# First attention of a four-layer block: the product of cosines and sines with the exponentials, on GpSimd or on VectorE

## What is computed

```python
p_w = exp(clip(score_scale * s_raw, -20, 20) + log_tw)     # per batch, position, channel
phi = k_val[..., None] * theta                             # 8 angles (M) per channel
re_k, im_k = cos(phi), sin(phi)
den    = cumsum(p_w, axis=1)                               # along the positions
num_re = cumsum(p_w[..., None] * re_k, axis=1)
num_im = cumsum(p_w[..., None] * im_k, axis=1)
...
out = sum over M of (num_re * A + num_im * B) / den        # A, B: from the queries
y   = silu(out * ...) @ W_out
```

## Time and profile before

| | |
|---|---|
| median of 3 runs | 1704.63 us (1704.37 to 1704.65) |
| the profiled execution, its own time | 1704.6 us |
| its span (first to last instruction) | 1702.8 us |
| VectorE busy over the span | 1182.2 us (69%) |
| TensorE busy, matmuls | 1216.5 us (71%) |
| ScalarE busy | 771.0 us (45%) |
| GpSimd busy | 417.0 us (24%) |

### The profile page before, as it was taken

How to read it: one execution, slowest core, us unless ns; L and a number is a source line. 1 busy time by engine, 2 the same in 40 slices (tenths; PEclk the granted TensorE clock), 3 DMA queues, 4 the chain that set the end, 5 groups by cost and what they waited for, 6 DMA issues and landing times. The chain is left out here.

```text
span 1702.8 us, 27530 instructions
## 1 busy us (share of the span) xinstructions
PE 1216.5 (71%) x8838; PEld 870.2 (51%) x8838; DVE 1182.2 (69%) x3159; ACT 771.0 (45%) x1217; POOL 417.0 (24%) x627
## 2 busy tenths in 40 slices
PE   2666566899986777755676774776665999967776
PEld 1555444788873333355343442665554344446665
DVE  4998899666666777544777675767874566647776
ACT  3334533233333766654466662433332466633333
POOL 3433443100003333011354431112220222100000
PEclk9888878899995999978789886878887799979998
DMA  7000000000000000000000000000000000000000
GB/s 279 1 0 0 0 0 0 1 0 0 0 0 1 2 0 1 2 0 0 1 1 0 1 1 0 1 0 0 1 0 1 1 2 0 2 1 0 0 0 25
DMA packets 5674, 13.83 MB, mean 8 GB/s; under 512 B 224, under 2 KB 4448, under 8 KB 5088
## 3 DMA queue, kind: packets, MB, share of 16 engines
q1 hardware_dynamic: 5600, 12.92, 2.0%
HBM read 11.88 MB, written 1.05 MB: 8 GB/s over the span
## 5 line engine op out<-in xcount | busy, mean ns | idle before, releaser
L1694 DVE TENSOR_REDUCE mx<-PS 128x2 f32<-128x512 f32 (+1 forms) x256 | 155.1, 620 | 82.7 <-PE PS L944 73.2
L359 POOL TENSOR_TENSOR tve<-tmv,eps 128x2 f32<-128x2 f32 x64 | 16.2, 253 | 720.3 <-DVE tmv L1480 719.1
L616 ACT ACTIVATE w_l0f<-PS 128x512 f32<-128x512 f32 (+1 forms) x256 | 137.3, 543 | 102.7 <-PE PS L951 100.4
L775 ACT ACTIVATE sg<-PS 128x512 f32<-128x512 f32 (+1 forms) x104 | 60.3, 580 | 201.0 <-PE PS L1391 200.7
L1391 PE MATMUL PS<-hT,w_l0f 128*128 128x256 f32 x512 | 121.4, 383 | 0.0
L870 PE MATMUL PS<-cb,w_const 128*128 128x256 f32 x128 | 44.6, 481 | 98.4 <-DVE sbuf L1620 98.3
L2101 DVE TENSOR_TENSOR y<-sg,PS 128x512 f32<-128x512 f32 (+1 forms) x104 | 69.2, 666 | 55.4 <-ACT sg L775 43.1
L815 PE MATMUL PS<-w_const,h 128*128 128x128 f32 x128 | 31.3, 331 | 98.2 <-DVE h L1471 88.6
L1391 PEld LDWEIGHTS PS<-hT,w_l0f 128*128 128x128 f32 x512 | 94.2, 193 | 10.8
L1320 PE MATMUL PS<-w_l2f,y 128*128 128x128 f32 x512 | 77.3, 300 | 10.3 <-ACT y L733 6.9
L1320 PEld LDWEIGHTS PS<-w_l2f,y 128*128 128x128 f32 x512 | 75.1, 216 | 17.9 <-ACT y L733 9.8
(11 more groups left out here) (369 smaller groups left out, 3348.1 us busy)
## 6 DMA issues: line engine op xcount, KB each, us to landing
w_l0f<-in_l0f SPq DMA_DIRECT2D x1, 3076.0 KB, 13.8
w_l2f<-in_l2f SPq DMA_DIRECT2D x1, 2214.0 KB, 19.8
w_l3f<-in_l3f SPq DMA_DIRECT2D x1, 1736.0 KB, 23.5
w_l0a<-in_l0a SPq DMA_DIRECT2D x1, 1093.0 KB, 7.9
result<-X SPq DMA_DIRECT2D x1, 896.0 KB, 4.6
X<-in_x SPq DMA_DIRECT2D x1, 768.0 KB, 10.2
w_l1f<-in_l1f SPq DMA_DIRECT2D x1, 582.0 KB, 15.5
PT<-in_cbf SPq DMA_DIRECT2D x1, 576.0 KB, 11.1
```

What stands on the lines that cost most here:

```text
L616: act.activation(P8[:, hh % 8, 0:width], PS[:, hh % 2, 0:width], ACT.Exp, scale=SM_SCALE).then_inc(a["pt"], 1)
L775: act.activation(sg[:, c % 2, 0:cols], gate, func).then_inc(f["sg"], 1)
L1694: dve.tensor_reduce(mx[:, hh, 0:nm], PS[:, 2 + hh % 2, 0:nm * keys].rearrange("p (t k) -> p t k", t=nm), AX.X, ALU.max).then_inc(a["mx"], 1)
```

## The change

GpSimd's loop for the first attention keeps only the two deviations. The two products of a chunk go to the head of VectorE's `cumulate`, which now waits for `a_trig` (and, for chunk 0, for `a_p`) instead of `a_pp`, issues the two products, raises `a_pp` itself (ScalarE still waits for it before it overwrites `pw`), and drains before the scans.

```diff
                 with pool.Fori(0, NB) as i:
                     if l == L0_ATTN:
-                        for c in range(CHUNKS):
-                            pool.wait_ge(a_trig, i * CHUNKS + (c + 1))
-                            if c == 0:
-                                pool.wait_ge(a_p, i + 1)
-                            for b in (cb, sbuf):
-                                ins = pool.tensor_tensor(b[:, c], b[:, c],
-                                                         pw[:].unsqueeze(1).to_broadcast([P, CHUNK_M, L]), ALU.mult)
-                            ins.then_inc(a_pp, 1)
-                            if c == 1:
-                                head_rstd(i + (head0[l] + 2))
+                        head_rstd(i + (head0[l] + 2))
                     tail_rstd(i + (tail0[l] + 1))
...
                     def cumulate(u, c):
-                        dve.wait_ge(a_pp, u * CHUNKS + (c + 1))
+                        dve.wait_ge(a_trig, u * CHUNKS + (c + 1))
+                        if c == 0:
+                            dve.wait_ge(a_p, u + 1)
+                        for b in (cb, sbuf):
+                            ins = dve.tensor_tensor(b[:, c], b[:, c],
+                                                    pw[:].unsqueeze(1).to_broadcast([P, CHUNK_M, L]), ALU.mult)
+                        ins.then_inc(a_pp, 1)
+                        dve.drain()
                         cf = carry[:].rearrange("p m t -> p (m t)")
```

## The result

| | before | after |
|---|---|---|
| median | 1704.68 us (15 runs, 1703.97 to 1709.90) | 1709.69 us (15 runs, 1702.92 to 1715.27) |
| ratio to before, 95% interval | | 1.0024 [1.0013, 1.0035] |
| profiled execution, its own time | 1704.6 us | 1710.82 us |
| its span | 1702.8 us | 1709.0 us |
| VectorE busy | 1182.2 us | 1177.0 us |

The account below looks back on a forecast made before the run. VectorE was taken as the busiest engine of the first attention (244.74 of 275 us), partly waiting beside GpSimd's products. -3.4 us on VectorE and +4.9 from TensorE's clock made +1.5 on 1704.6: 1706.1 us, range 1700.6 to 1712.0.

Parts of the forecast that it names:

- Added and freed: VectorE in a first-attention unit: products and drains add 5.44 us, vanished waiting frees 5.86, net -0.42, eight units -3.4 us.
- Deviations beside VectorE: GpSimd's deviations beside VectorE's first reduction: taken to cost 0, upper bound 0.69 us in each of eight units, +5.5 us.
- rival D: The deviations block VectorE in the first attention: 1706.7 us at most, with no clock fall; chance 0.10.
- The idle stretch before `sums` 3: TensorE's wait for chunk 3's products in each unit: grows from 1.39 to 3.1 us.
- TensorE's clock: At sums 3 the clock falls in every second of seven units: 3.5 falls at 1.4 us, +4.9 us.
- Rival A: TensorE's clock holds in all units of the first attention: 1701.2 us; chance 0.24.
- rival C: TensorE's clock falls at the wait for chunk 3's product in every unit: 1711.0 to 1713.8 us; chance 0.20.
- The end of the stage passes such a gain on whole: End of the first attention: the -3.4 us reaches the total whole, as the next layer starts behind the last `tail`.
- Rival E: The change doesn't free VectorE, whose long instructions are slow for another reason: +43 us, 1748 us; chance 0.04.

Follow-up runs that it names:

- filled: The changed kernel with five extra TensorE products between sums 2 and sums 3 in units 0 to 6; 1706.99 us, ratio 1.0004 to the kernel before.
- split version: The changed kernel with chunk 3's products put ahead of chunk 2's scans, same instructions; 1706.27 us, ratio 1.0001 to the kernel before.
- before + 26: The kernel before with 26 tiny VectorE instructions (13 memsets, 13 drains) ahead of VectorE's first wait; 1708.61 us, ratio 1.0007.

## Why the prediction was right or wrong

- **Added and freed.** Right in kind and nearly in size. A product is 0.68 us and the next starts 0.60 later. The drain costs 0.10, not 0.08 (107.27 + 0.68 to 108.05), and a whole chunk 6.11 us (105.56 to 111.67), not 6.06. A held unit is 34.36 us, so the net is -0.29 us per unit and not -0.42. Eight units gain 2.3 us, not 3.4; the 2.8 us of the filled and the split version hold another 0.5 from the last unit's clock.
- **Deviations beside VectorE: 0.** Right: VectorE's reduction stayed at 0.43 and 0.69, and rival D is out as a price. This doesn't show that the two engines never block each other. GpSimd's 0.69 became 0.85, and its `hve` of 0.19 took 1.10 until a scan of before ended, so it is the short operation that waits. The reason that I gave, that 128 x 2 elements hardly occupy anything, names only one of the two directions.
- **The idle stretch before `sums` 3.** I wrote 3.1 us, it is 3.00.
- **TensorE's clock.** "3.5 falls at 1.4 us, +4.9": the runs show three falls for 3.7 us, and five for 6.7, so 1.3 each, and 1.2 us more where the last unit fell again, which the prediction had as unchanged. The direction and the place of this term hold; that its sum is 4.8 us is luck. So is a part of the stage's +2.0 against +1.5: 1.1 us of gain too many in the sum met 1.2 us of falls too many. That units 0, 2 and 3 fell in two executions, and those and two more in the third, fits that what decides lies partly outside the program's order. Rival A happens when the stretch is closed, rival C in no profiled execution, not even with 3.40 us.
- **The step that didn't hold** is "The end of the stage passes such a gain on whole, since the next layer starts behind its last `tail`". The stage took 2.0 us longer than before and the profiled kernel 6.2 us. The seven later layers aren't a constant: their lengths differed by up to 9 us between kernels that don't differ in them. For the third feed-forward (+3.2) and the last attention (-3.1) it is shown that before + 26 has the lengths of the changed kernel, and in the first of them how 0.40 us come to 2.9 by way of the clock. These two cancel, though. What makes the sum, the second to fourth layers and the last (+3.4), grew as much in before + 26 (+4.0), which speaks for the place, but these layers vary between executions of one kernel too (1.7 us in the third layer, 1.0 in the last), and how much of the median's 5.0 us is theirs stays open. The timed runs of before + 26 put the place's share between -0.5 and +2.9 us.
- **Rival E** is out: everything that I had called waiting went away.

So the sign of the forecast was right for the reason given, the stage was met within 0.5 us, in part by errors that cancel, and the time was 3.6 us too low, for the most part because of a term that wasn't in the sum.

## What to carry to other kernels

Before work is moved off an engine that contends, look which instructions of the other engine stand beside it: beside factors from PSUM and a reciprocal the same products are free, and a version with one chunk of four placed there gained 0.59% where moving all of them lost 0.24%. When a reordering widens the space between two groups of matmuls, price the clock at both of its levels, and look for an order that splits the idle stretch in two. With a gain of 3 us in 1700, a kernel with idle instructions at its head is the control that is wanted: layers far behind an edit moved by as much.

## What the runs showed of the hardware

- An idle stretch of TensorE of 3.00 or 3.40 us in front of the same matmuls left the clock at 1.00 in some units and led to 0.50 in others of the same execution. In the filled and the split version, with stretches of 0.84 or 1.33 and 1.79 us, it held in all seven units. Where TensorE had run at half speed shortly before, in the last unit of the changed kernel, it fell behind 1.86 us of idle time. A fall made a unit 0.5 to 2.0 us longer.
- In two of the later layers VectorE idles some 0.4 us, waiting for nothing that the profile shows, only at places of its list that are 128 instructions or a multiple of it apart: 1349 or 1350, 1477, 1733, 1861, 2117 and 2245 in one kernel or another.
- 26 more instructions at the head of VectorE's list made a layer that starts 1000 us later 3.2 us longer and another 3.1 us shorter; with 64 more than before the first was as before.
- GpSimd's operation of 128 x 2 beside VectorE's reduction costs GpSimd 0.16 us and VectorE nothing, and beside a scan of 2.21 us it took 1.10 us instead of 0.19; its operation of 128 x 512 beside VectorE's reductions and scans costs VectorE 5.07 us per two chunks, and beside factors and a reciprocal nothing.
